# One sum with ones for two chunks of weights, in place of a maximum for each, and adapter groups in the even quads

## The reference

```python
def _L0_cond_ref(x, cond, norm_w, up_w, down_w):
    scale = cond @ norm_w.T + 1.0
    ms = jnp.mean(x * x, axis=-1, keepdims=True)
    h = x * (scale[:, None, :] * jax.lax.rsqrt(ms + EPS))
    u = h @ up_w.T                                  # 512 -> 2 * 2048
    val, gate = jnp.split(u, 2, axis=-1)
    h = val * jax.nn.gelu(gate, approximate=False)
    hq = h + jax.lax.stop_gradient(act_quant(h) - h)        # 8 bits, by row
    wq = down_w + jax.lax.stop_gradient(weight_quant(down_w) - down_w)
    return hq @ wq.T + x                            # 2048 -> 512

def _L1_cond_ref(x, h_lang, Wd, bd, Wu, bu, Wdd, bdd, Wdu, bdu):
    dWd = ((h_lang @ Wdd.T + bdd) * DELTA_SCALE).reshape(B, BN, D)
    dWu = ((h_lang @ Wdu.T + bdu) * DELTA_SCALE).reshape(B, D, BN)
    down = jax.nn.relu(jnp.einsum('bld,bnd->bln', x, Wd + dWd) + bd)
    return x + jnp.einsum('bln,bdn->bld', down, Wu + dWu) + bu
```

## Time and profile before

| | |
|---|---|
| median of three runs | 858.79 us (858.7 to 860.06) |
| the profiled execution | 857.9 us |
| its span | 856.1 us |
| TensorE busy | 843.4 us, 99% |
| VectorE busy | 610.6 us, 71% |
| ScalarE busy | 389.3 us, 45% |
| GpSimd busy | 77.1 us, 9% |

### The profile page before, as it was taken

The page is one execution under the profiler, slowest core; times in us unless marked ns, Lnnn a source line. Parts: engine busy times, 40 slices in busy tenths (PEclk is TensorE's granted clock), DMA queues, the critical chain, the costliest instruction groups (busy, mean ns, idle before and its releaser), DMA issues.

```text
span 856.1 us, 11930 instructions
## 1 busy us (share of the span) xinstructions
PE 843.4 (99%) x4026; PEld 373.2 (44%) x4026; DVE 610.6 (71%) x942; ACT 389.3 (45%) x632; POOL 77.1 (9%) x79
## 2 busy tenths in 40 slices
PE   6999999999999999999999999999999999999998
PEld 5344444444444444444444444444444444444443
DVE  5997877989887765567786555758986664445986
ACT  5778887766454541227445542126433332224000
POOL 0463322312000000000100000000200000000100
PEclk9999999999999999999999999999999999999999
DMA  9878888656899862367798863535247444432231
GB/s 347 321 255 314 306 313 283 236 189 216 294 355 372 308 231 99 111 231 275 279 330 309 282 223 102 178 117 179 92 135 234 136 160 133 144 107 85 98 124 74
DMA packets 64283, 183.50 MB, mean 214 GB/s; under 512 B 7008, under 2 KB 8032, under 8 KB 64224
## 3 DMA queue, kind: packets, MB, share of 16 engines
q1 hardware_dynamic: 63936, 182.48, 61.0%
q10 hardware_dynamic: 288, 0.26, 0.1%
HBM read 152.31 MB, written 29.36 MB: 212 GB/s over the span
## 4 chain that ended last, share of the span: by engine, by line
PE 89%; DVE 6%; issue 3%; ACT 2%; POOL 0%; DVEq 0%; ACTq 0%; POOLq 0%
PE aux_ps L1142 10%; PE b_ps L1053 9%; PE b_ps L1055 9%; PE b_ps L1057 9%; PE a_ps L1053 6%; PE a_ps L1055 6%; PE a_ps L1057 6%; PE aux_ps L1098 6%; PE aux_ps L1209 3%; PE aux_ps L1200 3%; PE c_ps L1053 3%; PE c_ps L1055 3%; PE c_ps L1057 3%; PE e_ps L1053 3%; PE e_ps L1055 3%; PE e_ps L1057 3%
## 5 line engine op out<-in xcount | busy, mean ns | idle before, releaser
L1550 DVE SCALAR_TENSOR_TENSOR h_ring<-v_sb,unscale,gelu 128x512 f32<-128x512 f32 x63 | 49.8, 790 | 103.0 <-ACT gelu L862 54.4
L838 ACT ACTIVATE b_ps<-a_ps 128x512 f32<-128x512 f32 x63 | 36.7, 582 | 146.6 <-PE a_ps L1057 146.4
L1053 PE MATMUL b_ps<-t_mov,u_l 128*128 128x512 f16 x252 | 95.5, 379 | 0.6 <-DVE c_ps L1511 0.6
L1057 PE MATMUL b_ps<-t_mov,u_l 128*128 128x512 f16 x252 | 95.5, 379 | 0.0
L1055 PE MATMUL b_ps<-t_mov,u_l 128*128 128x512 f16 x252 | 95.5, 379 | 0.0
L1574 DVE TENSOR_TENSOR hmax<-gelu,hmax 128x512 f32<-128x512 f32 x120 | 82.5, 688 | 7.0 <-ACT gelu L868 1.6
L1142 PE MATMUL aux_ps<-h_ring,wq 128*128 128x512 f16 x384 | 84.8, 379 | 0.0
L737 POOL PARTITION_ALL_REDUCE yscale<-hmax x8 | 17.9, 2267 | 603.4 <-DVE hmax L1574 602.7
L872 ACT ACTIVATE gelu<-h_ring 128x512 f32<-128x512 f32 x64 | 40.3, 630 | 54.8 <-DVE h_ring L1550 54.8
L868 ACT ACTIVATE gelu<-h_ring 128x512 f32<-128x512 f32 x64 | 40.3, 630 | 53.2 <-DVE h_ring L1560 52.5
L1560 DVE SCALAR_TENSOR_TENSOR h_ring<-b_ps,unscale,gelu 128x512 f32<-128x512 f32 x64 | 47.9, 748 | 21.1 <-PE b_ps L1057 21.1
(11 more groups left out here) (224 smaller groups left out, 1643.8 us busy)
## 6 DMA issues: line engine op xcount, KB each, us to landing
w_ring<-in_Wdu SPq DMA_DIRECT2D x64, 512.0 KB, 6.0
w_ring<-in_Wdd SPq DMA_DIRECT2D x56, 512.0 KB, 6.9
u_l<-ul_dram SPq DMA_DIRECT2D x48, 512.0 KB, 4.5
u_e<-ue_dram SPq DMA_DIRECT2D x48, 384.0 KB, 3.1
h_ring<-in_up_w SPq DMA_DIRECT2D x16, 512.0 KB, 6.3
x_sb<-in_x SPq DMA_DIRECT2D x8, 1024.0 KB, 8.3
res<-in_down_w SPq DMA_DIRECT2D x16, 512.0 KB, 7.3
ul_dram<-u_l SPq DMA_DIRECT2D x15, 512.0 KB, 5.1
```

Source lines behind the costliest of these rows:

```text
L1053: pe.matmul(ps[:, :], weight(n, p, 0, k), hi, start=fresh and k == 0, stop=False, skip_group_check=True)
L1057: mm = pe.matmul(ps[:, :], weight(n, p, 1, k), hi, start=False, stop=k == 1, skip_group_check=True)
L1550: dve.scalar_tensor_tensor(out=h_slot(n)[:, TB:TS], in0=val[:, :], scalar=unscale[:, s // 2, j:j + 1], in1=gelu2[:, :], op0=ALU.mult, op1= ...
```

## The change

The power of two no longer comes from the largest row sum but from the sum of all absolute values of the chunk. A product of a 128x128 matrix of ones with a column of `um` gives that sum on all 128 partitions at once, so transpose, reduction and spread go. The product takes two columns of `um`, for two chunks, and stands behind quads 2, 4, ..., 12, always in `e_ps` (chunks n + 2 and n + 3). In the head there is one for the condition (two columns) and chunk 0 in an `aux_ps` bank, one for chunks 1 and 2 in `e_ps` at the place of the old `bounds(-1)`, and one for chunk 3 behind quad 0. VectorE's `exponents` clamps and masks two columns from PSUM into the new tile `exps`, and two `u_scale` follow from there, at the head of quads 3, 5, ..., 13. The adapter groups of the first round move from quads 3, 5, ..., 15 to quads 2, 4, ..., 14. SyncE's loads for the groups of quad 17 come in quad 15.

```diff
-DW_QUADS = tuple(range(3, NP, 2)) + tuple(range(17, 26)) + tuple(range(30, 42))
+DW_QUADS = tuple(range(2, NP, 2)) + tuple(range(17, 26)) + tuple(range(30, 42))
...
-def bound_behind_groups(n):
-    return 1 <= n < NP - 2 and len(groups_of_quad(n)) > 0
+BOUND_QUADS = range(2, NP - 2, 2)
+def bound_count(j):
+    return 1 if j == 0 else 2 if j < 3 else j // 2 + 2
...
@@ side_work(n)
-    if n + 2 < NP and not bound_behind_groups(n):
-        work.append(("bounds", n))
+    if n == 0:
+        work.append(("bounds", 0))
...
@@ SyncE
-                if n > NP:
+                if n > NP + 1:
                     for g in groups_of_quad(n):
                         load_w(2 * g)
                         load_w(2 * g + 1)
...
@@ TensorE, product 5
-                    if bound_behind_groups(n - 1):
-                        pe.wait_ge(*bounds_read(n - 1))
+                    if n == 1:
+                        pe.wait_ge(s_top, bound_count(2))
+                    if n - 1 in BOUND_QUADS:
+                        pe.wait_ge(s_top, bound_count(n + 1))
...
@@ TensorE
             def first_bounds():
-                ps = take("turn", 0)
+                ps = take("total", 0)
+                pe.wait_ge(s_cm, 1)
+                pe.matmul(ps[:, 0:B], ones[:, :], cs_max[:, :], start=True, stop=True)
                 pe.wait_ge(s_um, 1)
-                pe.wait_ge(s_cm, 1)
-                for n, col in enumerate((cs_max[:, 0:1], cs_max[:, 1:2], um[:, 0:1])):
-                    mm = pe.transpose(ps[0:1, P * n:P * n + P], col, ident[:, :])
-                mm.then_inc(s_aux, 1)
-
-            def first_powers():
-                pe.wait_ge(s_top, 1)
-                pe.matmul(a_ps[1][:, 0:3], ones[0:1, :], um_top[0:1, 0:3], start=True,
-                          stop=True).then_inc(s_pow0, 1)
-
-            def bounds(n):
-                if bound_behind_groups(n):
-                    pe.wait_ge(s_p5sb, n)
-                    ps = e_ps
-                else:
-                    ps = take("bounds", n)
-                if n + 3 < NP:
-                    pe.wait_ge(s_um, n + 4)
-                    mm = pe.transpose(ps[0:1, 0:P], um[:, n + 3:n + 4], ident[:, :])
-                if n >= -1:
-                    pe.wait_ge(s_top, n + 3)
-                    mm = pe.matmul(ps[:, P:P + 1], ones[0:1, :], um_top[0:1, 0:1], start=True,
-                                   stop=True)
-                mm.then_inc(s_bounds if bound_behind_groups(n) else s_aux, 1)
+                pe.matmul(ps[:, B:B + 1], ones[:, :], um[:, 0:1], start=True, stop=True)\
+                    .then_inc(s_aux, 1)
+
+            def bounds(first, last, ps):
+                pe.wait_ge(s_um, last + 1)
+                return pe.matmul(ps[:, 0:last + 1 - first], ones[:, :], um[:, first:last + 1],
+                                 start=True, stop=True)
...
                 for g in groups_of_quad(n):
                     adapter_group(g)
-                if bound_behind_groups(n):
-                    bounds(n)
+                if n in BOUND_QUADS:
+                    pe.wait_ge(s_p5sb, n)
+                    bounds(n + 2, n + 3, e_ps).then_inc(s_total, 1)
...
@@ VectorE
-            def power(j):
-                if j == 0:
-                    aux_ready(dve, "turn", 0)
-                    ps, count = bank("turn", 0), 3
-                else:
-                    ps, count = bounds_ready(dve, j - 3), 1
-                top, bits = um_top[0:1, 0:count], um_top[0:1, 0:count].bitcast(I32)
-                row = ps[0:1, 0:P * count].rearrange("p (n m) -> p n m", n=count)
-                if j == 1:
-                    dve.wait_ge(s_pow0, 1)
-                link(dve.tensor_reduce(top, row, AX_X, ALU.max))
-                link(dve.tensor_scalar(top, top, 1e-30, None, ALU.max))
-                dve.tensor_scalar(bits, bits, EXP_MASK, None, ALU.bitwise_and).then_inc(s_top, 1)
+            def exponents(first, last, ps):
+                left = B + first if first else 0
+                top = exps[:, left:B + last + 1]
+                link(dve.tensor_scalar(top, ps[:, 0:B + last + 1 - left], 1e-30, None, ALU.max))
+                dve.tensor_scalar(top.bitcast(I32), top.bitcast(I32), EXP_MASK, None,
+                                  ALU.bitwise_and).then_inc(s_top, 1)
+                dve.wait_ge(s_top, bound_count(last))
...
-                if s == 0 and 1 < j and j + 1 < NP:
-                    u_scale(j + 1)
-                if s == 0 and 1 < j and j + 2 < NP:
-                    power(j + 2)
+                if n - 1 in BOUND_QUADS:
+                    dve.wait_ge(s_total, 1 + n // 2)
+                    exponents(n + 1, n + 2, e_ps)
+                    u_scale(n + 1)
+                    u_scale(n + 2)
```

More of the change, by code:

```diff
@@ L190, in up @@
         return [("up", i, k) for k in ks]
-    uses = [("scale", 0), ("stat", 0), ("turn", 0), ("bounds", -2)]
-    uses += [("dw", g) for g in range(4)] + [("bounds", -1)]
-    uses += [("dw", g) for g in range(4, EARLY)]
+    uses = [("scale", 0), ("stat", 0), ("total", 0)]
+    uses += [("dw", g) for g in range(EARLY)]
     for n in range(NQ):
@@ L240, in build @@
         small = sb("small", [P, 16])
-        cs_max, cs_pow, cs_mul = (small[:, B * n:B * n + B] for n in range(3))
-        um_top = small[:, 6:10]
+        cs_max, cs_mul = (small[:, B * n:B * n + B] for n in range(2))
         bd_sb, dsum, wmean, wmul = (small[:, n:n + 1] for n in range(10, 14))
@@ L246, in build @@
         um_mul = sb("um_mul", [P, NP])
+        exps = sb("exps", [P, B + NP])
         unscale = sb("unscale", [P, B, NP])
@@ L255, in build @@
         norm_raw = stage[:, 0, :]
+        cs_pow = exps[:, 0:B]
         h_half = h_ring[:, :, :].rearrange("p s t -> p (s t)").bitcast(F16).rearrange(
@@ L386, in build @@
         s_us = sem("s_us")
-        s_bounds = sem("s_bounds")
+        s_total = sem("s_total")
         s_first_hi = sem("s_first_hi")
@@ L415, in build @@
         s_stat1 = sem("s_stat1")
-        s_pow0 = sem("s_pow0")
         s_wq = sem("s_wq")
@@ L427, in aux_ready @@
             eng.wait_ge(s_aux, aux[key] + 1)
-        def bounds_read(n):
-            return (s_top, n + 4) if n + 3 < NP else (s_umul, 3 * (n + 2) + 3)
-        def bounds_ready(eng, n):
-            if bound_behind_groups(n):
[L434 to L437, removed]
         def bank_free(key):
@@ L445, in bank_free @@
                 "rs": (s_xs, KD * (i + 1)),
-                "turn": (s_top, 1),
-                "bounds": bounds_read(i),
+                "total": (s_top, 1),
+                "bounds": (s_top, bound_count(3)),
                 "mean": (s_mean, 1),
@@ L1224, in _ @@
             stat(0)
-            pe.wait_ge(s_const, 3)
             first_bounds()
             stat1(0)
+            pe.wait_ge(s_const, 3)
             spread_rs(0)
-            first_powers()
             stat1(1)
-            bounds(-2)
             stat1(2)
@@ L1242, in _ @@
             adapter_group(3)
-            bounds(-1)
+            pe.wait_ge(s_ms, 2)
+            bounds(1, 2, e_ps).then_inc(s_total, 1)
             pe.wait_ge(s_xs, 2 * KD)
@@ L1271, in _ @@
                     elif key[0] == "bounds":
-                        bounds(key[1])
+                        bounds(3, 3, take(*key)).then_inc(s_aux, 1)
                     elif key[0] == "mean":
@@ L1341, in scale_of, with u_multiplier, u_unscale @@
                                          float((254 + exp) * 2 ** 23), ALU.mult, ALU.add)
-            def u_multiplier(j, pow_):
-                scale_of(um_mul[:, j:j + 1], pow_, U_EXP).then_inc(s_umul, 1)
-            def u_unscale(j, pow_):
+            def u_multiplier(j):
+                scale_of(um_mul[:, j:j + 1], exps[:, B + j:B + j + 1], U_EXP).then_inc(s_umul, 1)
+            def u_unscale(j):
                 for b in range(B):
-                    dve.tensor_scalar(unscale[:, b, j:j + 1], pow_, 2.0 ** -(U_EXP + X_EXP),
-                                      cs_pow[:, b:b + 1], ALU.mult, ALU.mult).then_inc(s_umul, 1)
+                    dve.tensor_scalar(unscale[:, b, j:j + 1], exps[:, B + j:B + j + 1],
+                                      2.0 ** -(U_EXP + X_EXP), cs_pow[:, b:b + 1], ALU.mult,
+                                      ALU.mult).then_inc(s_umul, 1)
             def u_scale(j):
-                pow_ = bounds_ready(dve, j - 2)[:, P:P + 1]
-                u_multiplier(j, pow_)
-                u_unscale(j, pow_)
+                u_multiplier(j)
+                u_unscale(j)
             def u_low(j, part):
@@ L1406, in first_scales @@
             def first_scales():
-                dve.wait_ge(s_pow0, 1)
-                pow_ = a_ps[1]
-                u_multiplier(0, pow_[:, B:B + 1])
-                link(dve.tensor_scalar(cs_pow[:, :], pow_[:, 0:B], 1.0, None, ALU.mult))
+                u_multiplier(0)
                 link(scale_of(cs_mul[:, :], cs_pow[:, :], X_EXP))
@@ L1414, in second_scales @@
             def second_scales():
```

(15 more changed lines are left out.)

1 line of the change is left out of this document (removed).

## The result

The changed kernel takes 854.0 us (853.25 to 855.01, 4 runs), the kernel before beside it on the same chip 859.42 (858.7 to 861.15, 4 runs). The ratio is 0.9937, with a 95% interval of 0.9924 to 0.9951: 5.4 us less, 4.2 to 6.5. The profiled execution took 854.27 us with a span of 852.2.

The account below looks back on a forecast made before the run. TensorE was taken to bound the kernel after about 58 us, VectorE's order of work between 30 and 40 us. Gains of 4.6 us in the bound stretch and 1.6 in the head gave 6.2 less: 852.6 us, range 850.8 to 855.8.

Parts of the forecast that it names:

- The forecast case: Whole kernel: faster, 852.6 us, within 850.8 to 855.8; chance 0.60.
- The old step: Behind quads 2 to 13: transpose and product with ones, 0.51 us eleven times plus 0.31; removing them saves 5.9 us.
- the new pair: Behind quads 2, 4, ..., 12: one two-column product, 0.24 us each, six times, costs 1.44 us.
- The removed waits: Quads 4, 9 and 11: TensorE's waits for e_ps and ScalarE's copies vanish, saving 0.1 + 1.1 us.
- (a): Quad 6: squares' sum waits for ScalarE's copy behind two groups and the pair; costs 0.5 us, bounds 0.2 and 1.0.
- (b): After quad 10: next quad's product 5 waits for VectorE to take the exponents from e_ps; 0.3 us, bounds 0 and 0.8.
- (c): Turn to second round, quad 16: starts 1.94 us earlier against packed VectorE; waiting costs 0.3 us, bounds 0 and 1.5.
- The head: Up to quad 2's end: VectorE's shorter chain gains 1.2 us, a vanished wait 0.4; 1.6 in all, bounds 0.5 and 2.2.
- The 0.4 us that was to come from a wait for c_ps: Quad 2: VectorE loses 0.88 us of work, so TensorE's wait of 0.4 us there vanishes.
- Packed odd quads: Odd quads, above all 5 to 7 and 15 to 17: ScalarE and VectorE can't follow; 3.4 us back, 856.0 us; chance 0.15.
- Exponents late in every odd quad: Odd quads: VectorE's exponents late since every pair uses e_ps; slower than before, needing 1.3 us in each; chance 0.04.
- The head gives nothing: Kernel start: another chain, ScalarE's copies of the adapter groups, is as long; 854.2 us; chance 0.08.

Follow-up runs that it names:

- twenty products: Twenty unused products of ones on TensorE before its first products: added to the changed kernel 852.31 us, ratio 0.9925; added to the kernel before 860.49 us.
- the first pair of traces: Profiled executions of the kernel before and the changed kernel, no edit; 859.42 and 854.0 us. A second pair came from repeating both: 859.43 and 854.17 us.
- the version of all three: Changed kernel with second spread before first weight group, ScalarE's copy first in quad 6, VectorE's roots behind next quad's exponents; no products of ones: 852.29 us, ratio 0.9921.
- the sums alone: Changed kernel with the adapter groups back in the odd quads, pairs' sums still behind even quads: 858.53 us, ratio 0.9990.
- TensorE kept at work through the head: Changed kernel with 20 products of ones first, six in TensorE's idle time, one ahead of each eight one-column sums: 855.91 us, ratio 0.9960.

## Why the prediction was right, step by step

The forecast was 852.6 us in a range of 850.8 to 855.8; 854.0 was measured. As a difference that is 6.2 us forecast and 5.4 measured. The forecast case came about, though in the head not by the mechanism that was forecast.

**The old step** was costed at 0.51 us eleven times and 0.31 once, all on the path, the new pair at 0.24. The timeline shows 0.25 from pair to quad, and doubling it adds 0.22 to 0.23. Odd quads without a wait are 9.06 us long, quads 4, 8 and 10 are 11.25. Right. The upper bound of 0.43 came from rows of the head, eight instructions in 1.71 us; with twenty products ahead the same eight take 1.03.

**The removed waits**, 0.1 + 0.5 + 0.6, were read from the list of waits, which counts less than the gaps: by starts those of quads 9 and 11 were 0.59 and 0.68. Neither quad has such a wait now. The term was 0.2 too small.

**The new waits.** (a) Quad 6: 0.5 forecast, 0.69 measured, and taking the copy ahead of the absolute values removes it. (b) Quad 11: 0.3 forecast, 0.31 measured, and taking the roots out of VectorE's way removes it. (c) The turn to the second round: 0.3 forecast. TensorE's timeline between the starts of quads 17 and 18 shows distances of 0.27 us ahead of product 4 of quad 16, the one that was named, and 0.35 ahead of product 7 of quad 17, 0.2 in all over the usual 0.216:

```profile
209.04 0.38 PE L1053 MATMUL b_ps<-t_mov,u_e 128*128 128x512 f16 x1
209.31 0.38 PE L1049 MATMUL b_ps<-t_mov,u_l 128*128 128x512 f16 x1
...
211.68 0.38 PE L1053 MATMUL a_ps<-t_mov,u_l 128*128 128x512 f16 x1
212.03 0.38 PE L1049 MATMUL b_ps<-t_mov,u_l 128*128 128x512 f16 x1
```

The slack that VectorE had there, worked out from the earlier trace rows, was real. The stretch was forecast at 4.6 us and gave 5.04. Term (a) was 0.2 too low, and (c) 0.1 too high. Besides the removed waits, quad 13 gave 0.1 more than forecast, and an old step is 0.52 by the lengths of the quads.

**The head** is where the prediction failed: 1.6 us forecast, 0.38 in the first pair of traces and 1.40 in the second. The step that failed is "In that stretch VectorE's order of work sets the time, and TensorE's work there is mostly worth nothing by itself". The earlier trace rows already had TensorE busy for 9.81 of 10 us from 30 to 40, and from 14 us to quad 1 the changed kernel leaves it no gap: it is its work that counts.

The forecast followed VectorE. Its first scaled x was to come at 14.5 and came at 14.79, 0.92 us earlier than before in place of 1.2, and all of that lead went in the wait for the second spread. "At quad 1 the start is thus 1.2 us earlier" gave 0.07 and 1.20. The gain came from TensorE's steps instead, which the prediction counted as nothing: the first product starts 0.60 and 0.87 us earlier, and from the first weight group to quad 1 0.69 and 0.55 are saved.

Against that stand the twelve products at half speed. They cost 1.22 us more than before in the first pair and 0.22 in the second, since matmuls come to be 0.216 us apart at another time in each execution: 24.7 and 24.1 us in the changed kernel, 22.6 and 24.2 in the one before. The runs show the cost and not what sets that time.

The 0.4 us that was to come from a wait for c_ps "in quad 2" is in quad 1, and did not vanish. Quad 1 is shorter by 0.43 us (7.16 against 7.59) because the old step of 0.52 behind it is gone; its waits grew by 0.09. In quad 2 a new wait of 0.63 us for ScalarE's copy of a_ps stands in place of the old 0.23, and costs 0.12 net. Without the twelve products the first pair saves 0.60 + 0.69 + 0.43 - 0.12 = 1.6 us and the second 0.87 + 0.55 + 0.32 - 0.12 = 1.6. That this equals the forecast is luck: it is another sum. It was also close to all that could be had, since with TensorE 3.6 us ahead quad 1 starts 0.88 us earlier and no more.

**Behind quad 18** nothing was forecast, and nothing that belongs to the change is there. Quad 22 is longer than 11.94 by 0 and 0.6 us in the two traces of the kernel before and by 3.5 over quads 22 and 23 with only the groups moved; by 1.1 and 1.9 in those of the changed kernel, 0.2 with the copy first, 0.3 in the version of all three. The kernel before with the twenty products, which has none of the change, loses 3.0 us in quads 22 and 23 as well. The loads there thus land late with and without the change, and that it is chance is argued from that spread: no run shows its cause.

**The rivals.** Packed odd quads: fallen, quads 3, 5 and 7 are 9.06 us. Exponents late in every odd quad: fallen for the change as it is, but it is the case that came about in part with the sums alone, 1.35, 0.44 and 2.21 us in quads 3, 9 and 11. So its mechanism was the right one to fear, and the moved group is what keeps it away. The head gives nothing: nearly so in one execution, not in the other, and then through TensorE's half-speed products and not through ScalarE's copies.

## What to carry to other kernels

A cheaper way to a number pays only if the number still comes in time: here the cheaper sum gave 0.4 us by itself, moving the work that covers its consumer gave 0.1, and the two 5.1. Cost the head of a kernel on the engine that is never idle there, and follow another engine's lead to the next place where the two meet. Look behind that for the floor of the transfers. And a wait that hangs on an engine's order of work can go by swapping two entries, once the timeline says which entry the late one stood behind.

## What the runs showed of the hardware

The clock of TensorE in the head. In the changed kernel matmuls of 512 columns are 0.43 us apart until 24.7 us, yet the window gives a granted clock of 1.00:

```profile
20.00:22.00 2.00, 2.00 (x7) 0.65 (x5) 1.66 (x11) 2.00 (x3) 0.00 (x0) 1.00 1.02 406
```

With twenty products ahead the same stretch says 0.50, at the same spacing. So in the head a granted clock of 1.00 alone doesn't show that matmuls come at the closer spacing, and the spacing of like matmuls is what to read. Nor did a busy TensorE keep the clock: with TensorE kept at work through the head it is busy for all of 12 to 20 us, and yet the granted clock falls from 1.00 to 0.61 and 0.54 between 16 and 20 us. With the twenty products alone it is busy from 14 to 24 us, at 0.50 all that time.

Loads of 512 KB for the same quad land in very different times. The tile w_ring, loads for quad 22, changed kernel:

```profile
DMA to landing us min/median/max: 7.7/9.0/10.1
```

and in the kernel before, whose second execution has 7.2 to 9.6 for the same loads:

```profile
DMA to landing us min/median/max: 5.4/6.7/7.9
```
